# A Macaron block with a selective scan on one core: which slots' product with C run on GpSimd, and where the first FFN's statistics stand in VectorE's list

## The chip, the cores and the metric

One core of a Trainium2 chip. The metric is the device time of one execution in microseconds; the kernel before took 1582.62 us (median of 3 runs, 1580.9 to 1586.93). The engines are PE (TensorE), DVE (VectorE), ACT (ScalarE), POOL (GpSimd) and SP (SyncE, which issues the DMAs here).

## The reference, cut to what matters

x has 32 sequences of 256 tokens with 128 channels. Three residual steps follow each other:

```python
x = x + 0.5 * ffn(layernorm(x))          # first FFN, "f1"
x = x + mamba(layernorm(x))              # selective scan, "p"
x = x + 0.5 * ffn(layernorm(x))          # second FFN, "f2"

def ffn(x):                              # 8 experts, the gate picks one per token
    idx = argmax(softmax(x @ Wg + bg))
    h = gelu(x @ W1[e] + b1[e]); y = h @ W2[e] + b2[e]
    return y[idx]

def mamba(x):
    xn = rmsnorm(x) * norm_w
    xp, z = split(xn @ in_proj.T)        # 256 + 256 channels
    xp = silu(causal_conv4(xp) + conv_b)
    dt_x, B, C = split(xp @ x_proj.T)    # 128, 16, 16
    dt = softplus(dt_x @ dt_proj.T + dt_b)
    h_t = exp(dt_t * A) * h_(t-1) + dt_t * x_t * B_t     # 256 channels x 16 states
    y_t = sum_n h_t * C_t + D * x_t
    return (y * silu(z)) @ out_proj.T + x
```

## The kernel before, in words

The 8192 tokens are cut into 16 chunks of 512 (two sequences). The program is unrolled: every engine walks the same iterations i0 = -4 to 18 (`schedule`, line 162), and each iteration has 16 slots. The work of one chunk is spread over eight iterations. In iteration i0 the scan works on chunk i0; the first FFN's products on chunk i0+3; the norm of the scan's block and its first products on i0+2; z, B/C, dt on i0+1; the second FFN on i0-1 and i0-2; the store on i0-3. A stage is written as an offset, and `it.has(off)` leaves it out where no such chunk exists.

The scan itself: chunk i0 has 32 units of 128 partitions x 512 tokens, two in each slot. `place(s)` (line 115) gives a slot its half h of the channels, its group of states q and its part m. For each slot:

- POOL's `state_bx` (line 896) multiplies dt*x by B for both units at once (L904) into a ring `hb` of 8 slots. POOL does it two slots ahead: in its slot s it does bx of slot s+2.
- ACT's `decays` (line 589) writes exp(dt*A) into one of three PSUM banks dA (L605), one slot ahead. A bank comes free after the multiply of the unit that used it three units before, or already after that unit's scan, where the slot is one of POOL's.
- DVE's `state_unit` (line 715) scans (L727) and multiplies with C (L731), two of each per slot. In the slots named in `POOL_C` it only scans, into hb (L725), and POOL's `product_c` (line 907) multiplies both units with C in one instruction (L912). POOL reaches `product_c` for slot s in its slot s+1, behind bx of slot s+3.
- PE's `sum_states` (line 467) adds the states of two slots into Y with a selection matrix (L477). In its odd slot s it takes the pair (s-3, s-2): the pair 10 and 11 in slot 13, 12 and 13 in slot 15, 14 and 15 in slot 1 of the next iteration. It waits for DVE's and POOL's products.

What else stands in the slots is set by hand in tables (lines 48 to 67). Each engine runs its list in order; within a slot come first the stages at s, then the slot's own work, then those at s+0.5. What the change touches and what stands beside it:

- DVE: gated1 1.5 (L789), y_f2 2.0, gate_f1 3.0 (L758 to 769), out 5.5 (L783, X<-G: it adds the block's result from PSUM bank 0 and frees that bank), stats_f2 6.0, gated0 9.5, y_f1 10.0, stats_p 10.5, gate_f2 11.0, stats_f1 12.0, oh_f2 13.0, the convolution at 15.0 and 15.5 (L744). `norm_stats` (line 704) is 4 bn_stats, a one-element copy and 4 bn_aggr (L706, L710, L712).
- POOL: root_f2 6.5, norm_f2 7.0, dt 8.0, dtx 8.5, root_p 11.0, norm_p 12.0 (xr L887, then X L893), root_f1 12.5, norm_f1 13.0. root_p waits for stats_p.
- ACT: silu 4.0 (with its table load), copies of the experts' first products once a slot (L578), ln_p 13.5 (the copy of xrT, L569), taps 14.5, GELU of the second FFN 7.5 and of the first 15.5.
- PE: in slot 6 the product bc (L435, G<-xs,Wbc), which needs bank 0 that "out" used; dt1 in 6, dt0 in 7; in slot 13 the transposes ln_p (L427), in slot 14 x1 and x0 (L435, G<-xrT,Win). In each slot one first product of an expert (L446, L447 into PH) and one second product (L463 into PY). The order in slot 13 is ln_p, first product, sum of slots 10 and 11, second product; slot 14 begins with x1.
- SP: x_out 3 (stores chunk i0-3), x_in 4 (loads x), bc 6, then the fetches of B, C, dt and dtx. X is a ring of 8 chunks (`XR`). `fetch_c` waits until both engines' products that read the old C are done.

```python
# body of PE
for s in range(SLOTS):
    stages(it, s, 0)
    first_product(it, s)
    stages(it, s, 1)
    if s % 2 == 1 and s > 1 and it.has(0):
        sum_states(it, 0, (s - 3) // 2)
    second_product(it, s)
```

Of the kernel before, what the change touches and what calls it, by code (L numbers as in the profile page):

```python
# [18 lines left out]
J = CH // P  # L19
# [18 lines left out]
XR = 8  # L38
# [17 lines left out]
ACT_AT = {"ln_f1": 1.5, "silu": 4.0, "bc": 6.0, "dt1": 6.5, "dt0": 7.0, "soft": 7.0, "gelu_f2": 7.5,  # L56
          "ln_f2": 9.5, "ln_p": 13.5, "taps": 14.5, "gelu_f1": 15.5}
DVE_AT = {"gated1": 1.5, "y_f2": 2.0, "gate_f1": 3.0, "out": 5.5, "oh_f1": 6.0, "stats_f2": 6.0, "gated0": 9.5,
          "y_f1": 10.0, "stats_p": 10.5, "gate_f2": 11.0, "stats_f1": 12.0, "oh_f2": 13.0, "tap01": 15.0, "tap2": 15.5}
POOL_AT = {"root_f2": 6.5, "norm_f2": 7.0, "dt": 8.0, "dtx": 8.5, "root_p": 11.0, "norm_p": 12.0, "root_f1": 12.5,  # L60
           "norm_f1": 13.0}
SP_AT = {"x_out": 3, "x_in": 4, "bc": 6, "b0": 8, "dt": 9, "b1": 10, "c0": 10, "b2": 12, "c1": 12, "b3": 14, "dtx1": 14,
         "c2": 14, "dt1": 15, "c3": 15}
# [4 lines left out]
LN_OFF = {0: 3, 1: -1}  # L68


POOL_C = (1, 3, 5, 9, 14)
NP = len(POOL_C)
NV = UN - 2 * NP

# [30 lines left out]
def on_pool(s):  # L105

    return sum(m in POOL_C for m in range(s))


def on_dve(u):  # L110

    return sum(m // 2 not in POOL_C for m in range(u))

# [54 lines left out]
def macaron_kernel(nc, x, winT, wx, wxT, wdtT, woT, norm_w, conv_w, conv_b, dt_b, a_log, d_param,  # L168
# [3 lines left out]
    with ExitStack() as ctx:  # L172
        def sb(name, shape, dt=F32):
            return ctx.enter_context(nc.sbuf_tensor(name, shape, dt))
# [4 lines left out]
        def sem(name):  # L179
            return ctx.enter_context(nc.semaphore(name))  # L180

        X = sb("X", [P, XR * J, H])
# [76 lines left out]
        x_in = sem("x_in")  # L259
        x_out = sem("x_out")  # L260
# [4 lines left out]
        moments = [sem(f"moments_{w}") for w in names]  # L265
# [55 lines left out]
        def _(sp_):  # L321
            xd = x.rearrange("(t p) h -> p t h", p=P)
# [5 lines left out]
                sp_.dma_start(dst, src).then_inc(rest_in, 16)  # L328

            def load_x(it):  # L330
                dst, src = X[:, it.tiles(4), :], xd[:, J * (it.i0 + 4):J * (it.i0 + 5), :]
                it.wait(sp_, x_out, 4 - XR, 16, 16)
                it.wait(sp_, x_in, 4, 16, 0)
                sp_.dma_start(dst, src).then_inc(x_in, 16)

            def store_x(it):
                dst, src = od[:, J * (it.i0 - 3):J * (it.i0 - 2), :], X[:, it.tiles(-3), :]
                it.wait(sp_, y_added[1], -3, 1, 1)
                sp_.dma_start(dst, src).then_inc(x_out, 16)

            def store_bc(it):
                it.wait_read(sp_, g_free, "bc")
                sp_.dma_start(bc_dram[(it.i0 + 1) % 2], bcT[:, :]).then_inc(bc_stored, 16)

            def fetch_b(it, q):

                it.wait(sp_, bc_stored, 1, 16, 16)
                it.wait(sp_, bx, 0, SLOTS, 10 + 2 * q)
                rows = bc_dram[(it.i0 + 1) % 2, 0:N, :].rearrange("(n q) t -> q n t", q=NQ)[q]
                sp_.dma_start(bs[:, q, :], rows[None, :, :].broadcast_to([D32, N // NQ, CH])).then_inc(b_in[q], 16)  # L350

            def fetch_c(it, q):

                s = 10 + 2 * q
                it.wait(sp_, prod, 0, NV, on_dve(2 * s))
                it.wait(sp_, prod_p, 0, NP, on_pool(s))
                it.wait(sp_, bc_stored, 1, 16, 16)
                rows = bc_dram[(it.i0 + 1) % 2, N:2 * N, :].rearrange("(n q) t -> q n t", q=NQ)[q]
                sp_.dma_start(cs[:, q, :], rows[None, :, :].broadcast_to([D32, N // NQ, CH])).then_inc(c_in[q], 16)

            def store_dt(it):
                c = (it.i0 + 1) % 2
                it.wait(sp_, dtx_ready, 1, 1, 1)
                for h in range(HF):
                    sp_.dma_start(dtx_dram[c, :, h], dtx[:, h, :]).then_inc(dtx_stored[h], 16)
                it.wait(sp_, dt_ready, 1, 1, 1)
                for h in range(HF):
                    sp_.dma_start(dt_dram[c, :, h], dt[:, h].rearrange("p b l -> p (b l)")).then_inc(dt_stored[h], 16)
# [4 lines left out]
            def fetch_dtx(it, h):  # L373

                it.wait(sp_, bx, 0, SLOTS, 8 * (h + 1))
                it.wait(sp_, dtx_stored[h], 1, 16, 16)
                sp_.dma_start(dtx_rep[:, h].rearrange("p g t -> p (g t)"), copies(dtx_dram, (it.i0 + 1) % 2, h)) \
                    .then_inc(dtx_in[h], 16)

            def fetch_dt(it, h):  # L380

                it.wait(sp_, decay, 0, UN, SLOTS * (h + 1))
                it.wait(sp_, dt_stored[h], 1, 16, 16)
                sp_.dma_start(dt_rep[:, h].rearrange("p g t -> p (g t)"), copies(dt_dram, (it.i0 + 1) % 2, h)) \
                    .then_inc(dt_in[h], 16)

            def body(it):
                for s in range(SLOTS):
                    if s == SP_AT["x_out"] and it.has(-3):
                        store_x(it)  # L390
                    if s == SP_AT["x_in"] and it.has(4) and it.i0 + 4 > 0:
                        load_x(it)
                    if not it.has(1):
                        continue
                    if s == SP_AT["bc"]:
                        store_bc(it)
                    if s == SP_AT["b0"]:
                        fetch_b(it, 0)
                    if s == SP_AT["dt"]:
                        store_dt(it)  # L400
                        fetch_dtx(it, 0)
                        fetch_dt(it, 0)
                    for q in range(1, NQ):
                        if s == SP_AT[f"b{q}"]:
                            fetch_b(it, q)
                        if s == SP_AT[f"c{q - 1}"]:
                            fetch_c(it, q - 1)
                    if s == SP_AT["dtx1"]:
                        fetch_dtx(it, 1)
                    if s == SP_AT["dt1"]:  # L410
                        fetch_dt(it, 1)
                    if s == SP_AT["c3"]:
                        fetch_c(it, 3)
            schedule(body)
            sp_.wait_ge(x_out, 16 * NCH)
            sp_.wait_ge(bc_stored, 16 * NCH)
# [141 lines left out]
        def _(act):  # L558
# [30 lines left out]
            def decays(it, off, s):  # L589

                for u in (2 * s, 2 * s + 1):
# [7 lines left out]
                    else:  # L599
                        back, v = 1, [v for v in range(UN) if v % NA == u % NA][-1]  # L600
                    if v // 2 in POOL_C:
                        it.wait(act, scan, off - back, UN, v + 1)
# [67 lines left out]
        def _(dve):  # L670
# [31 lines left out]
            dve.wait_ge(zeroed, N_ZERO)  # L702

            def norm_stats(it, w, off):
                for j in range(J):
                    last = nc.vector.bn_stats(stat[:, w, j, :], X[:, it.tiles(off, j, 1), :])  # L706
                last.then_inc(stats[w], 1)
                it.wait(dve, stats[w], off, 1, 1)
                it.wait(dve, normed[w], off, 1, 0)
                nc.vector.tensor_copy(ticket[:, 1:2], ticket[:, 0:1])  # L710
                for j in range(J):
                    last = nc.vector.bn_aggr(mv[:, w, j, :], stat[:, w, j, :])  # L712
                last.then_inc(moments[w], 1)

            def state_unit(it, u):
# [7 lines left out]
                a = dA[u % NA][:, :]  # L723
                if s in POOL_C:
                    nc.vector.tensor_tensor_scan(x_in_hb, a, x_in_hb, 0.0, ALU.mult, ALU.add).then_inc(scan, 1)  # L725
# [66 lines left out]
            def stages(it, t):  # L792
# [22 lines left out]
                if t == DVE_AT["stats_f1"] and it.has(4):  # L815
                    it.wait(dve, x_in, 4, 16, 16)
                    norm_stats(it, 0, 4)
                if t == DVE_AT["stats_f2"] and it.has(-1):
                    it.wait_read(dve, g_free, "out")
                    norm_stats(it, 1, -1)  # L820
                if t == DVE_AT["stats_p"] and it.has(2):
                    it.wait(dve, y_added[0], 2, 1, 1)
                    norm_stats(it, 2, 2)
# [17 lines left out]
        def _(pool):  # L841
# [65 lines left out]
            def product_c(it, off, s):  # L907

                h, q, m = place(s)
                it.wait(pool, c_in[q], off, 16, 16)  # L910
                it.wait(pool, scan, off, UN, 2 * s + 2)
                nc.gpsimd.tensor_tensor(hb[:, s % HR], hb[:, s % HR], cs[:, q, None, :].broadcast_to([P, 2, CH]),  # L912
                                        ALU.mult).then_inc(prod_p, 1)
# [27 lines left out]
            def body(it):  # L941
                for s in range(SLOTS):
# [4 lines left out]
                    off, t = (0, s - 1) if s else (-1, SLOTS - 1)  # L947
                    if it.has(off) and t in POOL_C:
                        product_c(it, off, t)
# [49 lines left out]
```

## Time and profile before

| what | value |
|---|---|
| median of 3 runs | 1582.62 us (1580.9 to 1586.93) |
| the profiled execution | 1583.12 us, its span 1581.2 us |
| mean granted TensorE clock | 0.862 of full speed |
| HBM read and written | 106.94 MB and 22.02 MB, 82 GB/s over the span |
| chain that ended last, by engine | PE 43%, DVE 23%, ACT 22%, issue 7%, POOL 4% |

All times of the trace are microseconds from the span's start. In a row of a timeline stand the start, the length, the engine, the source line, the operation, output<-inputs, the shapes, how many instructions were merged, and in brackets how long the engine had been idle and what released it. The clock is given as a share of full speed: 1.00 is 2.4 GHz, 0.50 is 1.2 GHz. Examples are from the iteration i0 = 5 and its neighbours (about 584 to 688 us); the iterations from 2 to 12 look nearly alike. Unit numbers aren't in the rows: a slot on DVE is either two pairs of L727 and L731, or one merged row of L725.

### The profile page before, as it was taken

Reading aid. Unit: us, or ns where it says so; the run is one execution under the profiler, and the core shown is the slowest. Engines: PE = TensorE matmul, PEld = TensorE weight load, DVE = VectorE, ACT = ScalarE, POOL = GpSimd, SP = SyncE. Lnnn points to the kernel's source line nnn. Section 1 sums busy time; section 2 is a strip of 40 time slices with the busy share of each in tenths; the row PEclk is TensorE's granted clock in tenths of the full one; section 3 lists DMA queues with packets and bytes.
Section 4 is the critical chain, followed back from the end, with each engine's and each line's share of the span. In section 5 each row is a group of like instructions: output and inputs, shape, how many; then the busy total and the mean of one; then the engine's idle time right before and its main releaser. Section 6 shows DMA issues by size and latency. Waiting matters only on the chain.

```text
span 1581.2 us, 16257 instructions
## 1 busy us (share of the span) xinstructions
PE 1197.0 (76%) x5188; PEld 594.1 (38%) x5188; DVE 1063.0 (67%) x1713; ACT 876.8 (55%) x1171; POOL 1067.5 (68%) x900
## 2 busy tenths in 40 slices
PE   3777757597787868787777869877786868768677
PEld 1333414243433434343433434433443434324344
DVE  2022788867767687877777677777777686979920
ACT  0234646555665757465665746465665757474522
POOL 1026697958667777867777777877768777888610
PEclk9968778788897989989898989889898999788677
DMA  3005050503222220413222220413222230514000
GB/s 79 1 0 195 9 187 9 186 9 110 83 102 100 85 104 23 165 35 109 87 102 100 98 91 22 149 47 114 87 102 93 74 115 16 179 57 145 1 7 14
DMA packets 60405, 130.02 MB, mean 82 GB/s; under 512 B 7744, under 2 KB 26864, under 8 KB 52128
## 3 DMA queue, kind: packets, MB, share of 16 engines
q1 hardware_dynamic: 60320, 128.98, 23.8%
q8 instruction: 42, 0.69, 0.2%
q14 instruction: 43, 0.35, 0.1%
HBM read 106.94 MB, written 22.02 MB: 82 GB/s over the span
## 4 chain that ended last, share of the span: by engine, by line
PE 43%; DVE 23%; ACT 22%; issue 7%; POOL 4%; SPq 1%; ACTq 0%; DVEq 0%; DMA 0%; POOLq 0%
PE PH L447 11%; DVE dA L727 10%; PE PY L463 10%; PE G L435 8%; ACT hs L586 7%; PE Y L477 5%; DVE hb L731 4%; PE PH L446 3%; ACT dA L605 3%; ACT L587 3%; ACT hs L578 2%; DVE xs L744 2%; DVE hb L725 2%; ACT L586 2%; PE G L499 1%
## 5 line engine op out<-in xcount | busy, mean ns | idle before, releaser
L904 POOL TENSOR_TENSOR hb<-dtx_rep,bs 128x1024 f32<-128x1024 f32 x256 | 598.1, 2356 | 0.4 <-PE Y L477 0.4
L727 DVE TENSOR_TENSOR_SCAN dA<-dA,hb 128x512 f32<-128x512 f32 x352 | 429.3, 1220 | 60.6 <-ACT dA L605 56.4
L605 ACT ACTIVATE dA<-dt_rep,A 128x512 f32<-128x512 f32 x512 | 342.0, 690 | 205.8 <-DVE hb L731 195.4
L578 ACT COPY hs<-PH 128x512 f32<-128x512 f32 x256 | 149.7, 585 | 388.1 <-PE PH L447 387.7
L463 PEld LDWEIGHTS PY<-W,hs 128*128 128x128 f32 x2048 | 286.5, 207 | 172.3 <-issue 161.2
L463 PE MATMUL PY<-W,hs 128*128 128x128 f32 x2048 | 338.0, 306 | 0.0
L447 PE MATMUL PH<-xnT,W 128*128 128x512 f32 x512 | 333.0, 736 | 0.0
L912 POOL TENSOR_TENSOR hb<-hb,cs 128x1024 f32<-128x1024 f32 x80 | 188.5, 2356 | 175.9 <-DVE hb L725 175.9
L725 DVE TENSOR_TENSOR_SCAN hb<-dA,hb 128x512 f32<-128x512 f32 x160 | 186.8, 1209 | 135.2 <-ACT dA L605 132.5
L731 DVE TENSOR_TENSOR hb<-dA,cs 128x512 f32<-128x512 f32 x352 | 243.5, 692 | 25.2 <-DVE dA L727 0.9
L446 PE MATMUL PH<-ohT,Lm 24*128 24x512 bf16 x256 | 108.9, 425 | 158.0 <-ACT hs L578 157.5
L477 PE MATMUL Y<-hb,Sel 128*32 128x512 f32 x1024 | 168.3, 732 | 14.2 <-DVE hb L731 7.6
L446 PEld LDWEIGHTS PH<-ohT,Lm 24*128 24x128 bf16 x256 | 23.6, 92 | 274.0 <-ACT hs L578 188.8
L849 POOL TENSOR_SCALAR neg<-mv 128x4 f32<-128x4 f32 x48 | 9.6, 201 | 165.4 <-DVE mv L712 165.3
L586 ACT ACTIVATE hs<-hs 128x2048 f32<-128x2048 f32 x64 | 118.7, 1902 | 0.4
L744 DVE SCALAR_TENSOR_TENSOR xs<-G,Wc,xs 128x506 f32<-128x506 f32 (+2 forms) x96 | 67.3, 742 | 70.7 <-ACT xs L620 68.4
L447 PEld LDWEIGHTS PH<-xnT,W 128*128 128x128 f32 x512 | 85.9, 211 | 68.3 <-issue 68.3
L931 POOL TENSOR_TENSOR dt<-dt,sp 128x1024 f32<-128x1024 f32 x16 | 37.6, 2348 | 97.2 <-ACT sp L649 97.2
L519 PE MATMUL G<-Wg,xnT 128*128 128x8 f32 x256 | 40.6, 286 | 57.5 <-ACT xnT L569 57.5
L783 DVE SCALAR_TENSOR_TENSOR X<-PY,X 128x512 f32<-128x512 f32 x32 | 22.1, 690 | 75.8 <-PE PY L463 75.8
L427 PE MATMUL G<-Id,xn 128*128 128x128 f32 x128 | 25.3, 332 | 56.5 <-DVEq L748 54.2
L477 PEld LDWEIGHTS Y<-hb,Sel 128*32 128x32 f32 x1024 | 22.6, 117 | 120.2 <-issue 93.9
(85 smaller groups left out, 1180.7 us busy)
## 6 DMA issues: line engine op xcount, KB each, us to landing
dtx_rep<-dtx_rows SPq DMA_DIRECT2D x32, 1024.0 KB, 6.7
dt_rep<-dt_rows SPq DMA_DIRECT2D x32, 1024.0 KB, 8.2
bs<-bc_rows SPq DMA_DIRECT2D x64, 256.0 KB, 3.6
cs<-bc_rows SPq DMA_DIRECT2D x64, 256.0 KB, 4.5
dtx_rows<-dtx SPq DMA_DIRECT2D x32, 256.0 KB, 2.5
dt_rows<-dt SPq DMA_DIRECT2D x32, 256.0 KB, 2.6
X<-in_x SPq DMA_DIRECT2D x16, 256.0 KB, 3.1
out<-X SPq DMA_DIRECT2D x16, 256.0 KB, 2.4
```

What stands on the lines that cost most here:

```text
L446: nc.tensor.matmul(PH[:, :], Lm[:, e, :], ohT[:, w, :], start=True, stop=False)
L447: nc.tensor.matmul(PH[:, :], W1[:, e, :], xnT[:, w, :], start=False, stop=True).then_inc(ph_full, 1)
L463: last = nc.tensor.matmul(PY[:, P * j:P * (j + 1)], hs[:, w, e, P * j:P * (j + 1)], W2[:, e, :], start=False, stop=e == E - 1 and j == J - 1)
L477: last = nc.tensor.matmul(Y[D32 * g:D32 * (g + 1), :], Sel[:, :], hb[:, (2 * k + g // 2) % HR, g % 2], start=False, stop=q == NQ - 1)
L578: nc.scalar.copy(hs[:, w, e, :], PH[:, :]).then_inc(ph_free, 1)
L586: nc.scalar.activation(a, a, ACT.Gelu).then_inc(gelu[w], 1)
L605: nc.scalar.activation(dA[u % NA][:, :], dt_rep[:, h, g, :], ACT.Exp, scale=A[:, h, g, q:q + 1]).then_inc(decay, 1)
L725: nc.vector.tensor_tensor_scan(x_in_hb, a, x_in_hb, 0.0, ALU.mult, ALU.add).then_inc(scan, 1)
L727: nc.vector.tensor_tensor_scan(a, a, x_in_hb, 0.0, ALU.mult, ALU.add).then_inc(scan, 1)
L731: nc.vector.tensor_tensor(x_in_hb, a, cs[:, q, :], ALU.mult).then_inc(prod, 1)
L904: nc.gpsimd.tensor_tensor(hb[:, s % HR], dtx_rep[:, h, 2 * m:2 * m + 2, :], bs[:, q, None, :].broadcast_to([P, 2, CH]), ALU.mult).then_inc ...
L912: nc.gpsimd.tensor_tensor(hb[:, s % HR], hb[:, s % HR], cs[:, q, None, :].broadcast_to([P, 2, CH]), ALU.mult).then_inc(prod_p, 1)
```

## The change

`POOL_C` names five slots before and after. Before: 1, 3, 5, 9, 14. After: 3, 9, 11, 12, 14. So the multiplies of slots 1 and 5 go from POOL to DVE, those of 11 and 12 from DVE to POOL. The statistics of the first FFN (for chunk i0+4) go from the start of DVE's slot 12 to the end of its slot 2, in front of gate_f1. Since they are needed earlier, x is loaded one chunk sooner: in slot 4 SP now loads chunk i0+5, into the place of chunk i0-3, whose store it issued in slot 3, so the load waits for that store. `norm_stats` gets one more wait, on its own aggregates of the chunk before.

```diff
-          "y_f1": 10.0, "stats_p": 10.5, "gate_f2": 11.0, "stats_f1": 12.0, "oh_f2": 13.0, "tap01": 15.0, "tap2": 15.5}
+          "y_f1": 10.0, "stats_p": 10.5, "gate_f2": 11.0, "stats_f1": 2.5, "oh_f2": 13.0, "tap01": 15.0, "tap2": 15.5}
...
-POOL_C = (1, 3, 5, 9, 14)
+POOL_C = (3, 9, 11, 12, 14)
...
             def load_x(it):
-                dst, src = X[:, it.tiles(4), :], xd[:, J * (it.i0 + 4):J * (it.i0 + 5), :]
-                it.wait(sp_, x_out, 4 - XR, 16, 16)
-                it.wait(sp_, x_in, 4, 16, 0)
+                dst, src = X[:, it.tiles(5), :], xd[:, J * (it.i0 + 5):J * (it.i0 + 6), :]
+                it.wait(sp_, x_out, 5 - XR, 16, 16)
+                it.wait(sp_, x_in, 5, 16, 0)
...
-                    if s == SP_AT["x_in"] and it.has(4) and it.i0 + 4 > 0:
+                    if s == SP_AT["x_in"] and it.has(5) and it.i0 + 5 > 0:
...
             def norm_stats(it, w, off):
+                it.wait(dve, moments[w], off, 1, 0)
                 for j in range(J):
```

## Rows read from the trace of the kernel before

**Rows 1.** The page, part 1: each engine's busy time, share and instructions.
```profile
PE 1197.0 (76%) x5188; PEld 594.1 (38%) x5188; DVE 1063.0 (67%) x1713; ACT 876.8 (55%) x1171; POOL 1067.5 (68%) x900
```
**Rows 2.** Timeline of PE, 600 to 692 us: the z0 product, two iterations.
```profile
599.70 1.02 PE L435 MATMUL G<-xrT,Wz 128*128 128x512 f32 x2
...
688.39 1.02 PE L435 MATMUL G<-xrT,Wz 128*128 128x512 f32 x2
```
**Rows 3.** Chain that ended last, 600 to 700 us: start, length, what.
```profile
639.98 1.23 DVE dA L727
...
657.83 0.69 ACT dA L605
```
**Rows 4.** Timeline of DVE: slots 3, 5, 6, 7, 8, the addition out, and gated1 (L789).
```profile
601.45 2.34 DVE L725 TENSOR_TENSOR_SCAN hb<-dA,hb 128x512 f32<-128x512 f32 x2 [0.21 <-DVE oh L769]
...
610.00 2.34 DVE L725 TENSOR_TENSOR_SCAN hb<-dA,hb 128x512 f32<-128x512 f32 x2 [2.43 <-ACT dA L605]
612.26 0.67 DVE L783 SCALAR_TENSOR_TENSOR X<-G,X 128x512 f32<-128x512 f32 x1
...
614.41 1.20 DVE L727 TENSOR_TENSOR_SCAN dA<-dA,hb 128x512 f32<-128x512 f32 x1
...
618.18 1.22 DVE L727 TENSOR_TENSOR_SCAN dA<-dA,hb 128x512 f32<-128x512 f32 x1
...
625.76 1.23 DVE L727 TENSOR_TENSOR_SCAN dA<-dA,hb 128x512 f32<-128x512 f32 x1 [3.70 <-ACT dA L605]
...
682.96 0.69 DVE L789 TENSOR_TENSOR y<-Y,zs 128x512 f32<-128x512 f32 x1 [1.63 <-PE Y L477]
```
**Rows 5.** Timeline of DVE: start of stats_f1 and start of slot 12 behind it.
```profile
650.43 0.86 DVE L706 BATCH_NORM_STATS2 stat<-X 128x6 f32<-128x128 f32 x4
...
651.68 1.20 DVE L727 TENSOR_TENSOR_SCAN dA<-dA,hb 128x512 f32<-128x512 f32 x1
```
**Rows 6.** Timeline of POOL, root_p, xr, bx of slot 14, root_f1.
```profile
645.20 0.20 POOL L849 TENSOR_SCALAR neg<-mv 128x4 f32<-128x4 f32 x1 [6.39 <-DVE mv L712]
...
651.51 1.75 POOL L887 TENSOR_SCALAR xr<-X,neg,rms 128x128 f32<-128x128 f32 x4
...
655.08 2.37 POOL L904 TENSOR_TENSOR hb<-dtx_rep,bs 128x1024 f32<-128x1024 f32 x1
657.41 0.21 POOL L849 TENSOR_SCALAR neg<-mv 128x4 f32<-128x4 f32 x1
```
**Rows 7.** Timeline of PE, slot 13, x1 of slot 14, the sum in slot 15.
```profile
653.31 0.66 PE L427 MATMUL G<-Id,xr 128*128 128x128 f32 x4 [2.61 <-POOL xr L887]
...
655.27 1.07 PE L477 MATMUL Y<-hb,Sel 128*32 128x512 f32 x8
656.27 1.16 PE L463 MATMUL PY<-W,hs 128*128 128x128 f32 x8
659.09 1.13 PE L435 MATMUL G<-xrT,Win 128*128 128x512 f32 x2 [1.66 <-ACT xrT L569]
...
664.64 1.06 PE L477 MATMUL Y<-hb,Sel 128*32 128x512 f32 x8
```
**Rows 8.** Product with C on POOL and on DVE, ns min/median/max, first and last.
```profile
L912 POOL TENSOR_TENSOR hb<-hb,cs x80: 2337/2356/2368, 164.3 to 1502.3; 128x1024 f32<-128x1024 f32 x80
...
L731 DVE TENSOR_TENSOR hb<-dA,cs x352: 691/692/694, 157.8 to 1505.3; 128x512 f32<-128x512 f32 x176
```
**Rows 9.** Timeline of ACT: the exponentials for slot 4.
```profile
602.67 1.31 ACT L605 ACTIVATE dA<-dt_rep,A 128x512 f32<-128x512 f32 x2
```
**Rows 10.** Timeline of PE: the B/C product of slot 6.
```profile
613.52 1.90 PE L435 MATMUL G<-xs,Wbc 128*32 128x512 f32 x4
```
**Rows 11.** Busy time by stretch: us, PE, PEld, DVE, ACT, POOL, clock, DMA, GB/s.
```profile
631.90:638.70 6.80, 5.38 (x15) 1.78 (x16) 3.03 (x3) 4.86 (x8) 6.80 (x3) 0.50 0.85 306
474.90:481.70 6.80, 6.56 (x20) 2.62 (x21) 6.63 (x9) 2.99 (x5) 6.52 (x12) 0.50 0.21 73
```
**Rows 12.** The page, part 6: issues, KB each, median us to landing.
```profile
out<-X SPq DMA_DIRECT2D x16, 256.0 KB, 2.4
```

## The prediction

> **What bounds the kernel now.** I read the page's busy shares first: PE is busy 76% of the span, DVE 67%, POOL 68%, ACT 55% [rows 1], so no engine binds throughout and the question is who waits for whom in which slot. In the PE timeline the same product (z0, slot 1) of two consecutive iterations stands at 599.70 and 688.39: one full iteration takes 88.69 us, 5.5 us per slot [rows 2]. About eleven of the sixteen chunks run at that pace. The chain of what ended last, read over this iteration, changes hands [rows 3]: PE carries it from slot 1 to the dt products of slot 7, ACT carries it through softplus and the first GELU, and from 639.98 to 657.8 it is DVE's, slots 10 to 13, until ACT's exponentials, waiting for DVE's multiplies, release the copy of xrT and with it PE's product x1. Then come the taps, DVE's slot 15 and ACT's second GELU. The stretch of DVE is what the change unloads; what it loads is POOL behind slot 10 and DVE in slots 1 to 5. So I follow those two.
>
> **Part 1, DVE loses multiplies in slots 11 and 12.** A slot with both multiplies on DVE takes 618.18 - 614.41 = 3.77 us, a slot with them on POOL 612.26 - 610.00 = 2.26 [rows 4]: 1.51 us less in each. The statistics of the first FFN leave slot 12: 651.68 - 650.43 = 1.25 us [rows 5]. DVE is thus 4.3 us faster between slot 11 and slot 13, in the stretch that is on the path. ACT's waits for those multiplies go too, since a bank of dA behind a POOL slot is free after the scan. This alone would let xrT be copied some 1.2 us earlier (where ACT then waits only for PE's slot 13 and its own two exponentials); it can't be more, because PE reaches x1 no earlier than 656.27 + 1.16 = 657.43, against 659.09 now [rows 7].
>
> **Part 2, POOL gets them, in slots 12 and 13 of its own list.** POOL idles 6.39 us at root_p, waiting for DVE's stats_p, and nothing of the change moves that moment (645.20). From there POOL works without a break: root_p, bx of slot 13, xr at 651.51, the update of X, bx of slot 14 from 655.08 until 657.41 [rows 6]. Only then, by the program's order, does it come to the product with C for slot 11, new here, at 2.356 us [rows 8]: ready at 659.8. PE wants exactly that product in its slot 13 (the sum of slots 10 and 11), which it starts at 655.27 [rows 7]. So PE, which is in order, stands 4.5 us longer, and behind it are queued the second product of slot 13, x1, the first product of slot 14 and x0. The sum and the second product take 2.1 us together, so x1 starts at 659.8 + 2.1 = 661.9 instead of 659.09: **+2.8 us**, and the 1.66 us that PE used to wait for xrT have been swallowed. ACT's copy of slot 14, its taps, DVE's convolution and slot 15 and the GELU follow x1 directly, so all of it is passed on. Of DVE's 4.3 us nothing reaches the end. The product for slot 12 comes two POOL operations (norm_f1, bx 15) after root_f1, at about 667.7; PE asks for it in slot 15 at 664.64 + 2.8 [rows 7], a wait of 0.3 at most, which I cost at nothing (cover: the delay just counted). The products of slots 9 and 14 stay where they were. norm_p runs in the fourteen iterations that have a chunk two ahead: 14 x 2.8 = **39 us**.
>
> By the Trainium skill (GPSIMD Engine Reference, Elementwise side-by-side cycle accounting) a two-input elementwise operation on GpSimd takes 1.96 times as long as on VectorE. Here the trace does not agree for this size: 2356 ns against two of 692 ns is 1.70 [rows 8]. By the page's ratio the product would take 2.71 us and the total would be 5 us higher.
>
> **Part 3, DVE gets more in slots 1 to 5.** Slot 1 grows by 1.51 us; it ends before PE's sum of slots 14 and 15, for which DVE waits 1.63 us there anyway [rows 4], so nothing. The statistics come in between slot 2 and gate_f1: 1.25 us. gate_f1 is asked for by PE only three slots later, nothing. But slot 3 starts 1.25 later: 602.7 instead of 601.45, its first scan ends at 603.9, and ACT's second exponential of the pair at 602.67, which needs that bank, ends at 604.6 instead of 603.98 [rows 4, 9]: ACT is 0.65 late into the silu block, which it runs without a break up to the exponential that DVE waits 2.43 us for at slot 5. So slot 5 starts 0.65 late and is itself 1.51 longer, now that its multiplies are DVE's: the addition "out" (612.26) comes 2.16 us later. It frees PSUM bank 0 for PE's B/C product of slot 6, which started at 613.52, that is 0.59 us after out had ended at 612.93 [rows 4, 10]. PE, the carrier of the path here, stalls 2.16 - 0.59 = **1.6 us**, and dt1, dt0, softplus and the GELU behind it move with it. Slots 6 and 7 on DVE end 2.2 late at 624.2, before slot 8, whose exponentials let DVE wait 3.70 us until 625.76 [rows 4] and now come 1.6 later still, so no more is lost. Thirteen iterations have both steps: 13 x 1.6 = **21 us**.
>
> **Part 4, the clock.** PE now waits 2.61 us at 653.31 for xr, works 3 us and would then stand for 4.5 us more [rows 7]. After waits of this kind the granted clock falls to half: 631.9 to 638.7 while PE waits out the GELU, and once in this very place, 474.9 to 481.7, after the wait for xr alone [rows 11]. The low stretch is 6.8 us long both times, all of it full of work in the second. Price: nothing if the clock holds, 3.4 us if all 6.8 us fall on work. I take 2.0, since the first part passes while PE still stands, in twelve iterations: **24 us**.
>
> **Part 5, loads and waits.** The load of x moves one chunk ahead and now waits behind the store just issued: 2.4 us on the SP queue at slot 4 [rows 12]. Behind it on SP is the store of B/C, two slots (11 us) later; nothing, and if that cover were gone, 2.4 us an iteration. SP's fetches of C wait for POOL's products now (659.8 and 667.7): next use is over 20 us away. The added wait on moments is for something DVE finished a chunk earlier: 0, at most a few hundredths per use. In the last two chunks there is no norm_p and DVE binds: slots 1 and 5 cost 3.0 us there, slots 11 and 12 give 3.0 back; 0, within 3 either way.
>
> **Sum.** 1583.1 (the profiled run; its span is 1581.2, the median of the runs 1582.6) + 39 + 21 + 24 = **1667 us**.
>
> **The rivals.**
> (a) The clock holds through the double wait: for it, the iteration of rows 7 held it after 2.61 us (at half clock the one matmul group at 655.27 would take nearly double); against it, the wait is now 4.5 and comes right behind another. 1583 + 39 + 21 = 1643. Chance 0.20.
> (b) Only one of the two stalls is real, most likely because out is not late: ACT's silu block may absorb the 0.65, or PE be late itself. 1583 + 39 = 1622 with the clock high, 1646 with it low; 1604 for out alone. Chance 0.11.
> (c) The low clock lasts over the whole of slots 13 and 14 and the product for slot 12 also holds PE: 3.4 instead of 2.0 and 0.3 more, 1688. Chance 0.07.
> (d) **Faster**: POOL delivers the product for slot 11 before PE asks. Then DVE's gain counts, x1 starts at 657.8 instead of 659.09: 14 x 1.2 = 17 us, 1566 us. It decides at 655.3: POOL would have to be through bx 14 by 652.9, 4.5 us sooner than in rows 6, and root_p starts no sooner since stats_p does not. For it speaks that DVE's stretch is the path now; against it every duration in rows 6. Chance 0.08.
> (e) Both effects small and cancelling: the gain of (d) against the stall at out, 1583 + 21 - 17 = 1587, within 0.5%. Chance 0.04.
>
> **How the numbers follow.** Chances: forecast 0.50, the rivals as given. The range reaches from 1618, just under (b)'s 1622, to 1692, just over (c); that leaves out (d), (e) and a bit of (b). A measurement of this kernel can tell about 0.5%, 8 us, from no change. Faster by more than that: 0.08; within: 0.04; slower: the rest, 0.88.
>
> **What would show it.** Right: an iteration of about 95 us instead of 88.7; in the waits PE's Y (line 477) waiting for POOL's hb (the product with C) about 4.5 us a chunk where it was 6.5 us in all, and ACT's wait for DVE's multiplies much smaller; PE's B/C product waiting for DVE's X about 1.6 us a chunk; the clock at half around slots 13 and 14. Wrong: if PE starts x1 before 659 in this frame, part 2 falls; if the wait for X is missing, part 3; if matmuls of slot 13 keep their length, part 4. An iteration under 88 us would show (d).

## The result, and the profile after

The changed kernel takes 1673.01 us (median of 4 runs, 1671.4 to 1673.88) against 1582.34 us for the kernel before: a ratio of 1.0567, 95% interval 1.0544 to 1.0590. Its profiled execution has a span of 1669.5 us, 88.3 us more than the 1581.2 of before. The forecast was 1667, in a range of 1618 to 1692.

The page of the changed kernel, part 1 and the chain that ended last. The lines behind line 704 of the kernel have moved down by one.

```profile
PE 1215.3 (73%) x5188; PEld 599.1 (36%) x5188; DVE 1065.7 (64%) x1713; ACT 874.0 (52%) x1171; POOL 1064.8 (64%) x900
...
PE 31%; ACT 23%; DVE 20%; POOL 15%; issue 10%; SPq 1%; DVEq 0%; ACTq 0%; DMA 0%; POOLq 0%
```

Against [rows 1] PE is busy 18 us more and no other engine more than 3 us; PE's 18 us are slower matmuls, not more of them. POOL's busy time has not grown, but its share of the chain went from 4% to 15%. Same work, other order: the time lies in waits.

The timeline of PE in the changed kernel, one iteration (i0 = 5), from z0 to the z0 of the next, with the places of [rows 2, 7, 10]:

```profile
631.96 1.02 PE L435 MATMUL G<-xrT,Wz 128*128 128x512 f32 x2
...
647.41 1.88 PE L435 MATMUL G<-xs,Wbc 128*32 128x512 f32 x4 [1.49 <-DVE X L784]
...
686.69 0.66 PE L427 MATMUL G<-Id,xr 128*128 128x128 f32 x4 [2.58 <-POOL xr L888]
...
693.23 1.94 PE L477 MATMUL Y<-hb,Sel 128*32 128x512 f32 x8 [4.52 <-POOL hb L913]
695.10 2.08 PE L463 MATMUL PY<-W,hs 128*128 128x128 f32 x8
696.97 1.91 PE L435 MATMUL G<-xrT,Win 128*128 128x512 f32 x2
...
727.54 1.02 PE L435 MATMUL G<-xrT,Wz 128*128 128x512 f32 x2
```

An iteration is 727.54 - 631.96 = 95.58 us long, against 88.69 [rows 2]. Two waits of PE are new: 1.49 us for the addition out ahead of the B/C product, and 4.52 us for POOL's product with C ahead of the sum of slots 10 and 11, where there was no wait at all [rows 7]. The sum then takes 1.94 us instead of 1.07, the second product 2.08 instead of 1.16. That is the half clock: the granted clock is 0.50 from 692.0 to 698.8, a stretch of 6.8 us that begins 1.2 us before the sum. Every steady iteration of the changed kernel has three such stretches (6.8, 6.8 and 10.2 us); in the kernel before most have two, and the one at slot 13 is missing. The wait of 1.66 us for xrT ahead of x1 is gone.

POOL's timeline there, the counterpart of [rows 6], and the windows of busy time around PE's resumption (columns as in [rows 11]):

```profile
678.62 0.20 POOL L850 TENSOR_SCALAR neg<-mv 128x4 f32<-128x4 f32 x1 [5.95 <-DVE mv L713]
...
684.89 1.74 POOL L888 TENSOR_SCALAR xr<-X,neg,rms 128x128 f32<-128x128 f32 x4
...
688.44 2.35 POOL L905 TENSOR_TENSOR hb<-dtx_rep,bs 128x1024 f32<-128x1024 f32 x1
690.74 2.35 POOL L913 TENSOR_TENSOR hb<-hb,cs 128x1024 f32<-128x1024 f32 x1
```

```profile
683.20:690.00 6.80, 2.94 (x16) 1.53 (x14) 5.46 (x7) 2.98 (x6) 6.70 (x10) 1.00 0.11 39
...
693.20:697.00 3.80, 3.77 (x17) 2.13 (x18) 0.03 (x1) 0.00 (x0) 3.62 (x8) 0.50 0.29 73
```

POOL is busy from 678.62 on without a gap, in the old order, with the new product at its end. DVE meanwhile stands: in its timeline slot 14 waits 1.99 us for bx and then the taps are 9.64 us away. That is where the multiplies taken from DVE went.

```profile
690.89 2.34 DVE L726 TENSOR_TENSOR_SCAN hb<-dA,hb 128x512 f32<-128x512 f32 x2 [1.99 <-POOL hb L905]
702.87 2.72 DVE L745 SCALAR_TENSOR_TENSOR xs<-G,Wc,xs 128x506 f32<-128x506 f32 x4 [9.64 <-ACT xs L620]
```

The waits of the whole run (who waited for whom, us in total, times, longest):

```profile
PE Y L477 <- POOL hb L913: 68.8, 19, 5.9
...
PE G L435 <- DVE X L784: 22.0, 14, 3.3
```

In the kernel before the same two were 6.5 us (2 times) and 2.6 us (2 times).

### The profile page after: what moved, and what is told of

Read it like the earlier page. It is cut to its first block, busy times and chain, and to the rows that moved or that the text cites. A ratio compares the mean times of both kernels' runs of the same rounds, so it can differ in the third digit from the quotient of the medians.

```text
span 1669.5 us, 16301 instructions
## 1 busy us (share of the span) xinstructions
PE 1215.3 (73%) x5188; PEld 599.1 (36%) x5188; DVE 1065.7 (64%) x1713; ACT 874.0 (52%) x1171; POOL 1064.8 (64%) x900
## 4 chain that ended last, share of the span: by engine, by line
PE 31%; ACT 23%; DVE 20%; POOL 15%; issue 10%; SPq 1%; DVEq 0%; ACTq 0%; DMA 0%; POOLq 0%
DVE dA L728 9%; PE PH L447 8%; PE PY L463 8%; PE G L435 7%; ACT hs L586 7%; POOL hb L905 5%; PE Y L477 5%; DVE hb L732 3%; ACT dA L605 3%; ACT hs L578 3%; POOL hb L913 3%; ACT L587 2%; PE PH L446 2%; ACT L586 2%; DVE xs L745 2%
## 5 line engine op out<-in xcount | busy, mean ns | idle before, releaser
L605 ACT ACTIVATE dA<-dt_rep,A 128x512 f32<-128x512 f32 x512 | 341.0, 690 | 173.1 <-DVE hb L732 125.3
L463 PEld LDWEIGHTS PY<-W,hs 128*128 128x128 f32 x2048 | 292.2, 211 | 180.7 <-issue 169.8
L463 PE MATMUL PY<-W,hs 128*128 128x128 f32 x2048 | 344.7, 310 | 0.0
L447 PE MATMUL PH<-xnT,W 128*128 128x512 f32 x512 | 329.3, 729 | 0.0
L913 POOL TENSOR_TENSOR hb<-hb,cs 128x1024 f32<-128x1024 f32 x80 | 188.2, 2352 | 141.7 <-DVE hb L726 141.6
L477 PE MATMUL Y<-hb,Sel 128*32 128x512 f32 x1024 | 177.0, 767 | 72.3 <-POOL hb L913 68.8
L519 PEld LDWEIGHTS G<-Wg,xnT 128*128 128x128 f32 x256 | 40.2, 234 | 71.5 <-ACT xnT L569 65.7
```

The lines of the kernel that those rows point to most:

```text
L447: nc.tensor.matmul(PH[:, :], W1[:, e, :], xnT[:, w, :], start=False, stop=True).then_inc(ph_full, 1)
L463: last = nc.tensor.matmul(PY[:, P * j:P * (j + 1)], hs[:, w, e, P * j:P * (j + 1)], W2[:, e, :], start=False, stop=e == E - 1 and j == J - 1)
L477: last = nc.tensor.matmul(Y[D32 * g:D32 * (g + 1), :], Sel[:, :], hb[:, (2 * k + g // 2) % HR, g % 2], start=False, stop=q == NQ - 1)
L605: nc.scalar.activation(dA[u % NA][:, :], dt_rep[:, h, g, :], ACT.Exp, scale=A[:, h, g, q:q + 1]).then_inc(decay, 1)
```

## The experiments

Ratios are against the kernel before, timed beside each; the iteration is read in the steady part (z0 to z0, i0 = 5 to 11). "Low clock" is the sum of all recorded stretches with a granted clock of 0.50; the last of them reaches some 2 us beyond the span in every row.

| kernel | us | ratio, 95% interval | iteration, us | low clock, us |
|---|---|---|---|---|
| before | 1582 to 1586 | 1 | 88.7, some 90 to 91 | 440 |
| changed | 1673.0 | 1.0567 (1.0544 to 1.0590) | 95.58 | 498 |
| e1, slots only | 1673.7 | 1.0564 (1.0529 to 1.0599) | 95.57 | 502 |
| e2, statistics only | 1580.2 | 0.9975 (0.9956 to 0.9993) | 88.51, 89.86, 87.88 in turn | 454 |
| e3, without slot 11 | 1582.7 | 0.9990 (0.9971 to 1.0008) | 88.75 | 410 |
| e4, second half only | 1638.9 | 1.0341 (1.0307 to 1.0375) | 94.71 and 93.02 in turn | 501 |
| e5, out before slot 5 | 1646.3 | 1.0393 (1.0366 to 1.0420) | 94.72 and 93.01 in turn | 488 |
| e6, root_p later | 1635.8 | 1.0327 (1.0301 to 1.0353) | 92.16 | 528 |
| e7, PE kept busy | 1648.2 | 1.0409 (1.0383 to 1.0434) | 94.75 and 92.98 in turn | 460 |
| e8, candidate | 1531.3 | 0.9666 (0.9638 to 0.9694) | 85.33 | 410 |
| e9, before, root_p later | 1598.5 | 1.0086 (1.0066 to 1.0105) | 91.22, 91.60, 90.24 in turn | 470 |
| e10, candidate, old slots | 1573.1 | 0.9931 (0.9907 to 0.9956) | 88.75 | 439 |
| e11, second candidate | 1509.3 | 0.9521 (0.9502 to 0.9541) | 83.34 and 83.91 in turn | 379 |
| e12, changed, both repaired | 1628.6 | 1.0275 (1.0252 to 1.0298) | 92.16 | 502 |

### The parts of the change alone

**e1**, the kernel before with one line of the change:

```diff
-POOL_C = (1, 3, 5, 9, 14)
+POOL_C = (3, 9, 11, 12, 14)
```

> The kernel before with only POOL_C changed; the statistics stay in slot 12 and x is loaded as before. Theory (the product for slot 11 reaches PE 4.5 us late and PE's clock falls behind it; the addition out comes late): the wait of Y for POOL's hb stays about 4.6 us a chunk; in the first half slot 5 is no longer 0.65 us late but still 1.5 longer, so PE's B/C product stands 0.9 instead of 1.6 us. An iteration of 94.8 us, in all 1664 us. Rival (the moved statistics and the earlier load do the harm, by holding gate_f1 and SP): near 1582 us.

The whole loss is there without the statistics: 1.0564 against 1.0567. The rival is dead. But 9 us less were expected, and the step that was to give them did happen. In the changed kernel the B/C product starts 15.45 us behind z0, in e1 14.94, 0.5 sooner (13.82 in the kernel before). Its row:

```profile
646.91 1.88 PE L435 MATMUL G<-xs,Wbc 128*32 128x512 f32 x4 [1.05 <-DVE X L783]
```

The 0.5 us are lost again piece by piece further on: 15.56 instead of 15.31 from the softplus (ACT's second pass, L649) to y_f1 (DVE's addition of the first FFN's result), 14.63 instead of 14.46 from x1 to the GELU, 16.20 instead of 16.12 from there to the next z0. Those are the parts with the three low stretches, which stand in both kernels at the same places behind z0 (to 0.2 us) while e1's work comes sooner; their sum over the run is 3 us longer. Both iterations end at 95.57 to 95.58.

**e2**, the changed kernel with `POOL_C = (1, 3, 5, 9, 14)`: only statistics and load moved.

> The changed kernel with the five old slots: only the statistics and the load of x are moved. Theory: DVE is 1.25 us faster in slots 11 to 13, which is the path there, and 0.65 us later at slot 5, where 0.59 us of slack takes it: x1 starts up to 1.2 us earlier, an iteration of 87.5 us, 1566 us in all (14 times 1.2 less than 1582.6). Rival (statistics and load do the harm): 1640 us or more. Rival (the gain doesn't reach the end): 1582.

Slightly faster, by 0.25% (0.07 to 0.44); the harm is not here, and the 16 us of gain did not come either. The timeline of PE shows why. First an iteration as expected, x1 2.62 us behind the sum instead of 3.82, then another of the same kernel:

```profile
651.20 0.66 PE L427 MATMUL G<-Id,xr 128*128 128x128 f32 x4 [2.57 <-POOL xr L888]
653.16 1.07 PE L477 MATMUL Y<-hb,Sel 128*32 128x512 f32 x8
655.78 1.13 PE L435 MATMUL G<-xrT,Win 128*128 128x512 f32 x2 [0.47 <-ACT xrT L569]
...
739.83 1.12 PE L427 MATMUL G<-Id,xr 128*128 128x128 f32 x4 [2.58 <-POOL xr L888]
743.41 1.94 PE L477 MATMUL Y<-hb,Sel 128*32 128x512 f32 x8
746.68 1.02 PE L435 MATMUL G<-xrT,Win 128*128 128x512 f32 x2
```

The same wait of 2.6 us ahead of ln_p leaves the clock high in one and low in the other (1.07 and 1.94 us for the same sum). Here the low one comes in every third iteration; in the kernel before it was an exception [rows 11]. The 1.2 us are earned in two of three iterations (from y_f1 to x1 18.49 us, 19.72 in the kernel before) and lost in the third (20.76). Of the two, one is 88.51 us long all the same, since 16.37 us lie between the GELU and z0, 15.63 in the kernel before. The mean of the three is 88.75.

**e4**, the changed kernel with slots 1 and 5 on POOL as well:

```diff
-POOL_C = (3, 9, 11, 12, 14)
+POOL_C = (1, 3, 5, 9, 11, 12, 14)
```

> The changed kernel with slots 1 and 5 back on POOL as well, seven slots in all: only the second half is changed, with the statistics in slot 2. Theory: out comes 0.65 late at most, so PE's B/C product starts as before; the wait for the product of slot 11 and the low clock stay whole: an iteration of 94 us, 1652 us. Rival (POOL as a whole is too full): slower than the changed kernel, over 1673, since POOL has 4.7 us more to do in each iteration.

POOL does 4.7 us more work in each iteration and the kernel is 34 us faster than the changed one, so POOL's load as such is not the cause; its order is. The B/C product is back at 13.87 us behind z0, the sum of slots 10 and 11 stays where it was. The gain was 13 us larger than expected. The steady iteration is not the place (93.87 us on average, 94 expected): most of it comes at the two ends of the run. Every second steady iteration (93.02) has 1.1 us less between x1 and the GELU, the clock again; the low stretch begins there before PE's transposes and not with the wait for the product, which is 2.88 us and not 4.51.

**e3**, the changed kernel with slot 11 on DVE: `POOL_C = (3, 9, 12, 14)`.

> The changed kernel with slot 11 left to DVE: four slots, 3, 9, 12 and 14. Theory: PE's slot 13 waits for no product of POOL, the granted clock holds there, x1 is reached up to 1.2 us earlier than in the kernel before, and only the 1.6 us at out stay: an iteration of about 89.1 us, 1588 us (1580 to 1595). Rival (any product of POOL behind norm_p holds the path, slot 12's too, by 2 us in slot 15): 1615 us or more.

One product fewer on POOL takes all of the 5.7% away (0.9990, not distinguishable from the kernel before), although the stall at out is still there (15.44 us to the B/C product). It came out 5 us below the value expected, inside its range. PE waits for no product in slot 13:

```profile
656.74 0.66 PE L427 MATMUL G<-Id,xr 128*128 128x128 f32 x4 [2.42 <-POOL xr L888]
659.10 1.93 PE L477 MATMUL Y<-hb,Sel 128*32 128x512 f32 x8
662.27 1.02 PE L435 MATMUL G<-xrT,Win 128*128 128x512 f32 x2
```

Slot 12's product, also behind norm_p, costs nothing in the end: PE waits 1.09 us for it in slot 15, and its next wait, ahead of the transposes of xn (L427), is 2.25 us where it was 3.41. The sum in this row is slow all the same, so "the clock holds there" was wrong; the copy of xrT, early now, lets x1 follow at 3.17 us in spite of it. What pays for the stall at out is the clock as well: the low stretch behind PE's wait for the GELU is 3.4 us long here and 6.8 in the kernel before, and from the softplus to y_f1 it is 0.9 us less. So e3 shows what the product for slot 11 costs together with the low stretches that it brings.

### The three terms, each taken away

**e5** moves one addition in DVE's list:

```diff
-          ... "gate_f1": 3.0, "out": 5.5, "oh_f1": 6.0 ...
+          ... "gate_f1": 3.0, "out": 5.0, "oh_f1": 6.0 ...
```

> The changed kernel with the addition out ahead of DVE's slot 5 (5.0 instead of 5.5), where DVE is idle for ACT. Theory: bank 0 is free when PE comes to its B/C product, so the 1.6 us a chunk go and nothing else changes in the second half: 94 us an iteration, 13 x 1.6 = 21 us less, 1652 us. Rival (PE would stand there for something else, the wait is only where the time shows): 1673, unchanged.

The wait of the B/C product is gone, and 27 us with it (21 expected). The wait of 4.5 us in the second half is still there in every iteration:

```profile
638.35 1.90 PE L435 MATMUL G<-xs,Wbc 128*32 128x512 f32 x4
...
684.57 1.94 PE L477 MATMUL Y<-hb,Sel 128*32 128x512 f32 x8 [4.53 <-POOL hb L913]
```

The low stretch that goes with it is 6.8 us long in one iteration (94.72 us) and 3.4 in the next (93.01). The steady iteration is thus 1.7 us shorter on average, close to the 1.6 expected; the rest of the 27 us comes at the two ends of the run.

**e6** lets POOL do bx of slot 13 before it waits for the statistics:

```diff
-POOL_AT = {..., "root_p": 11.0, "norm_p": 12.0, ...
+POOL_AT = {..., "root_p": 11.5, "norm_p": 12.0, ...
```

> The changed kernel with POOL's root_p behind bx of slot 13 (11.5 instead of 11.0): bx of slot 13 falls into the time in which POOL idles for the statistics, so the rest of POOL's list up to the product for slot 11 ends 2.3 us earlier. Theory: PE gets that product 2.3 us earlier and x1 with it; 14 x 2.3 = 33 us less, 1640 us if the clock still falls, 1612 if it now holds. Rival (the low clock alone makes the loss, its length is fixed): over 1660.

1635.8 us, 37 us less than the changed kernel and 4 below the value expected with a falling clock. The product with C reaches PE 2.1 us earlier (from the start of root_p to the sum 12.48 us, 14.61 in the changed kernel), and x1 starts as much earlier. The iteration is 3.4 us shorter, since less of what follows is slow (x1 to the GELU 13.76 us, 14.46 in the changed kernel; from there to z0 15.73 for 16.12). The low stretches of a steady iteration add up to the same 23.8 us; the 30 us more of low clock in the table lie before the steady part. PE's wait is as long as before, only the one ahead of it has shrunk, from 2.58 to 0.42 us:

```profile
678.35 0.66 PE L427 MATMUL G<-Id,xr 128*128 128x128 f32 x4 [0.42 <-POOL xr L888]
684.91 1.93 PE L477 MATMUL Y<-hb,Sel 128*32 128x512 f32 x8 [4.54 <-POOL hb L913]
```

So here the low clock comes with the second wait alone; the one for xr ahead of it is nearly gone.

**e7** keeps PE busy while it waits:

```diff
+WARM = 5
...
+                    if s == 13 and it.has(0) and it.has(2):
+                        it.wait_free(pe, g_free, "x1")
+                        for _ in range(WARM):
+                            nc.tensor.matmul(G[1][:, :], Win[:, 0:P], xnT[:, 0, :], start=True, stop=True)
                     if s % 2 == 1 and s > 1 and it.has(0):
                         sum_states(it, 0, (s - 3) // 2)
```

> The changed kernel with five spare fp32 products of 512 columns in PE's slot 13, ahead of the sum of slots 10 and 11, into the PSUM bank that x1 overwrites: they fill some 2.6 us of the 4.5 us that PE stands for POOL. Nothing is left out. Theory: the wait itself stays, but the granted clock holds at 1.00 there; what the low clock cost (x1 1.6 us after the sum, 0.8 up to the GELU, a little behind) comes back: 2.4 us an iteration, 93.2 us, 1643 us. Rival (the matmuls were not on the path, only the wait was): 1673.

More matmuls, and 25 us faster than the changed kernel. Two neighbouring iterations in PE's timeline (one line was added ahead of these, so L478 is the sum and L436 is x1; L554 are the spare matmuls, two instructions for each fp32 product):

```profile
679.85 6.08 PE L554 MATMUL G<-xnT,Win 128*128 128x512 f32 x10
685.87 1.06 PE L478 MATMUL Y<-hb,Sel 128*32 128x512 f32 x8
687.86 1.02 PE L436 MATMUL G<-xrT,Win 128*128 128x512 f32 x2
...
774.80 4.45 PE L554 MATMUL G<-xnT,Win 128*128 128x512 f32 x10
779.50 1.06 PE L478 MATMUL Y<-hb,Sel 128*32 128x512 f32 x8 [0.25 <-POOL hb L918]
781.50 1.02 PE L436 MATMUL G<-xrT,Win 128*128 128x512 f32 x2
```

The spare matmuls take 4.45 us at full clock, not the 2.6 expected, so they fill the wait almost to its end (0.25 us are left). The sum takes 1.06 us again and x1 follows it in 1.99 us instead of 3.73. In the first of the two the spare matmuls began in a low stretch, took 6.08 us and were themselves 1.4 us too long, which is the part that did not come back. The Trainium skill (TensorE: Matmul & The Clock Gate, HAM oscillation) describes a loop in which the clock falls again in each pass because PE waits for a DMA in it, and advises to restructure the loop so that PE stays at full speed. The runs agree for a wait on another engine: the changed kernel has the low stretch at slot 13 in each steady iteration, and with the wait filled the ratio is 1.0409 instead of 1.0567.

**e12**, the changed kernel with the edits of e5 and e6:

> The changed kernel with root_p at 11.5 and out at 5.0. Theory (two separate stalls in series): the two gains add, 37 and 27 us less than the changed kernel, 1609 us, an iteration of about 91 us; PE still waits 2.2 us for the product of slot 11. Rival (the clock swallows part of it): 1620 or more.

1628.6, not 1609: on top of e6 the repair of out brings 7 us and not 27. Its B/C product is 1.57 us earlier, 13.87 instead of 15.44, and its iteration is 92.16 us like e6's. The next parts took it back: softplus to y_f1 15.94 instead of 15.12 us, x1 to the GELU 14.27 instead of 13.76, GELU to z0 15.98 instead of 15.73. That is 0.82 + 0.51 + 0.25 = 1.58. The 7 us come from the first four iterations, before the steady part (6.4 us in the profiled runs). PE still waits 4.52 us for the product of slot 11, where 2.2 had been expected. The rival of that run, that the clock swallows part, was right.

### What bounded the kernel before

**e9** is the kernel before with the edit of e6.

> The kernel before with one edit: root_p behind bx of slot 13 (11.5). xr is ready 2.3 us earlier. Theory (in the kernel before DVE's slots 11 to 13 set x1, POOL does not): PE stops waiting for xr in slot 13 and waits as long for the copy of xrT instead; x1 stays, an iteration of 88.7 us, 1582 us, or a little less because the clock holds more surely. Rival (POOL's list behind the statistics is the bound before as well as after): 2.3 us an iteration less, 1550 us.

It is slower, by 0.86% (0.66 to 1.05), and neither side had said so. PE's timeline:

```profile
655.00 0.66 PE L427 MATMUL G<-Id,xr 128*128 128x128 f32 x4 [0.39 <-POOL xr L887]
...
656.96 1.06 PE L477 MATMUL Y<-hb,Sel 128*32 128x512 f32 x8
657.96 1.16 PE L463 MATMUL PY<-W,hs 128*128 128x128 f32 x8
663.00 1.68 PE L435 MATMUL G<-xrT,Win 128*128 128x512 f32 x2 [3.88 <-ACT xrT L569]
664.62 0.60 PE L446 MATMUL PH<-ohT,Lm 24*128 24x512 bf16 x1
665.15 1.95 PE L447 MATMUL PH<-xnT,W 128*128 128x512 f32 x2
```

The theory holds in its first half: POOL did not set x1 in the kernel before, DVE did through xrT, and PE merely waits elsewhere: 0.39 + 3.88 us instead of 2.61 + 1.66 [rows 7]. But the two short waits had mostly kept the clock, and the one long wait behind full work loses it in every steady iteration, now ahead of matmuls on the path (1.68 for x1 instead of 1.13, 1.95 instead of 1.12). Bringing a value early to an engine that must still wait for another made the iteration 1.5 to 2.9 us longer.

### Versions that beat both

**e8** gives DVE's stretch relief where POOL idles: slot 10's product runs while POOL waits for the statistics.

```diff
-POOL_C = (3, 9, 11, 12, 14)
+POOL_C = (1, 3, 5, 9, 10, 14)
...
-DVE_AT = {..., "out": 5.5, ...
+DVE_AT = {..., "out": 5.0, ...
...
-POOL_AT = {..., "root_p": 11.0, ...
+POOL_AT = {..., "root_p": 11.5, ...
```

> A version that should beat both: statistics of the first FFN in slot 2, out ahead of slot 5, root_p behind bx of slot 13, POOL_C = 1, 3, 5, 9, 10, 14. The product for slot 10 runs where POOL idles for the statistics, which come 1.5 us sooner. Theory: no new wait of PE for POOL, xr some 2 us earlier, DVE 2.8 us shorter between slots 10 and 13: x1 1.2 to 3 us earlier than in the kernel before, an iteration of 86 to 87.5 us, 1545 to 1566 us. Rival (DVE's stretch is not what sets x1): 1582.

1531.3 us, 14 us below the range given. PE finds xr and all products ready and waits only for xrT:

```profile
640.50 0.66 PE L427 MATMUL G<-Id,xr 128*128 128x128 f32 x4
...
642.46 1.06 PE L477 MATMUL Y<-hb,Sel 128*32 128x512 f32 x8
...
646.10 1.13 PE L435 MATMUL G<-xrT,Win 128*128 128x512 f32 x2 [1.49 <-ACT xrT L569]
```

**e10** is e8 with the five old slots.

> The candidate with the five old slots (1, 3, 5, 9, 14): tells what slot 10 on POOL is worth. Theory (DVE's stretch is the path): only the 1.25 us of the statistics are gained there, about 87.5 us an iteration, 1560 to 1568 us. Rival (the candidate's gain is that of xr and out): as the candidate, 1531.

1573.1 us, 5 us above the range. Slot 10 on POOL is worth 42 us, more than the 1.5 us a slot that DVE saves (14 x 1.5 = 21). The rest goes with the clock: in e10 PE waits longer for xrT (36.9 us in all, e8 21.1), a low stretch of 3.4 us follows in every steady iteration, which e8 does not have there, and 14.58 us lie between x1 and the GELU, 13.67 in e8.

**e11** adds two edits to e8:

```diff
-POOL_C = (1, 3, 5, 9, 10, 14)
+POOL_C = (1, 3, 5, 9, 10, 15)
...
-          ... "ln_p": 13.5 ...
+          ... "ln_p": 13.0 ...
```

> The candidate with two further edits of the same kind: ACT copies xrT at 13.0 instead of 13.5, ahead of the exponentials that wait for DVE, and slot 15 instead of 14 has its products on POOL, so that DVE's last slot before the GELU is 1.5 us shorter, while slot 14 falls into DVE's wait for the taps. Theory: x1 1.5 us earlier (PE waits 1.49 us for xrT there) and the GELU another 1.5 to 1.9: 82 to 83 us an iteration, 1490 to 1505 us. Rival (the clock gives the time back by longer low stretches): 1515 or more.

1509.3 us, 4.8% less than the kernel before. x1 now stands 1.99 us behind the sum, with no wait at all:

```profile
625.15 1.07 PE L477 MATMUL Y<-hb,Sel 128*32 128x512 f32 x8
...
627.14 1.02 PE L435 MATMUL G<-xrT,Win 128*128 128x512 f32 x2
```

It is 4 us above the range expected. From x1 to the GELU 0.7 us were won where 1.5 to 1.9 had been counted (12.95 for 13.67), and GELU to z0 is 16.33 us in every second iteration, 15.25 in e8.

## Why the prediction was right

- **Part 2, the product for slot 11.** Forecast: PE stands 4.5 us, x1 starts 2.8 us late. Measured: 4.52 us of wait. e3 takes away that one product and with it the whole loss (in part through the clock, as said there); e6 brings it 2.1 us earlier and x1 comes as much earlier. e4 shows that order and not load does it. That slots 12, 9 and 14 cost nothing was right as well: the sum in slot 15 of the changed kernel waits for nobody.
- **Part 1, nothing of DVE's gain reaches the end.** Right in the changed kernel (DVE idles 9.64 us before the taps). ACT's wait for DVE's multiplies fell from 195.4 to 125.3 us, while that for its scans rose from 8.5 to 46.9. e2 shows that the gain was real (x1 1.2 us earlier behind y_f1 in two of three iterations), and e9 that x1 did not hang on POOL before.
- **Part 3, out.** Forecast 1.6 us; from z0 to the B/C product 15.44 against 13.82 us, 1.62. Both halves of its working are there, though not in the sizes given: without the moved statistics (e1) the delay is 1.12 us where 0.92 was reckoned, so the part through ACT is 0.50 and not 0.65. The two errors cancel. e5 confirms where the delay sits. What it costs in the end is less fixed: 27 us on the changed kernel (e5), 7 on e6 (e12).
- **Part 4, the clock.** Forecast 2.0 us an iteration. Measured, part by part: sum to x1 3.73 where the warm work is 2.1, so 1.6; x1 to the GELU 14.46 for 13.67, 0.8; GELU to z0 16.12 for 15.63, 0.5; less 0.45 in the part behind the softplus (15.31 for 15.76). Together 2.5, and e7 gives 1.7 of it back on average. So this term was 0.5 too small; it was seen only behind the wait, whereas low stretches elsewhere shift too. The stretch itself is as it was priced, 6.8 us, of which 1.2 pass before PE resumes. It is also why the iteration is 95.6 and not 95.1, and why rival (a) was wrong.
- **Part 5, loads and waits.** Forecast nothing. e2 has the earlier load and the added wait and is not slower (0.9975).
- **The sum.** 84 us were forecast and 88 came in the span: from the first z0 to the last the changed kernel takes 91 us more, since the iterations are a little longer than reckoned, and the last two chunks gave 2 us back where the text said 0, within 3. That the sum came as near as 6 us is in part luck: in e1 0.5 us an iteration less did not show in the time at all, and in e12, on top of e6, 1.6 us did not show in the steady iteration.
- **The ratio of POOL to DVE.** The product took 2352 ns on average in the changed kernel (188.2 us for 80), nearly as before, which is 1.70 times two of DVE's 692 ns. The Trainium skill (GPSIMD Engine Reference, Elementwise side-by-side cycle accounting) has 1.96 for an addition of 2048 elements; the trace does not agree for this shape.
- What the prediction missed is that its terms don't simply add. It treated the clock as one more term. e1, e2 and e12 show it as something that answers every other term: 0.5 us, 1.2 us (in two of three) and 1.6 us an iteration were saved, and all or most of it was lost again in the parts that the low stretches cover. The sum came out because both waits were large against that.

## What to carry to other kernels

Before moving work to an engine with idle time, find where in its in-order list the new instruction will stand and who asks for the result when: here 2.35 us on an engine with a third of its time free kept PE standing for 4.5 us, while the same instruction one slot earlier, in the gap in front of a known wait, made the kernel 42 us faster (e8 against e10). A wait of TensorE must be costed with the matmuls behind it, and two short waits can be cheaper than one of the same sum (the kernel before against e9). Where a loop is paced like this, judge an edit by the whole iteration, and expect that savings of 0.5 to 1.6 us in it can vanish (e1, e2, e12) or count for more than their size (e6: 2.1 us made 3.4; e8 against e10: 1.6 made 3.4).

## What the runs showed of the hardware

- The granted clock ties parts of an iteration together that have no dependence on each other. Kernels whose work differs by 0.5 us (e1 and the changed kernel) or 1.6 us (e6 and e12) have the same iteration to 0.01 us (95.57 and 95.58; 92.16 twice), others alternate in a fixed rhythm of two or three (e4 and e5, made by different edits, both with 94.7 and 93.0). The steady iterations of one length are 85.33 us (e8), 88.75 (e3, e10), 92.16 (e6, e12) and 95.57 (the changed kernel, e1), in equal steps of 3.41 us with nothing between; the three lengths of e2 average 88.75 too, the pairs of e4, e5 and e7 93.87, half a step. What in the clock's control makes it so was not examined.
- Waits of the same length, 2.57 and 2.58 us, in one kernel (e2) left the clock high in one iteration and low in another. Waits of 3.88 us (e9) and 4.5 us (the changed kernel, e5, e6) went with half speed in every steady iteration (e5: for 3.4 and 6.8 us in turn).
- Spare matmuls can shorten a kernel: ten more instructions a chunk in a wait of 4.5 us, 25 us less than the changed kernel (e7).
